# A Swin transformer block on one core: attention output and MLP moved one iteration later, new PSUM banks and engine orders, bias vectors loaded as rows

## The reference

```python
xn = layernorm(x, ln1_w, ln1_b)
xw = windows(roll(xn, (-3, -3)))            # (1024 windows, 49 tokens, 192)
q, k, v = split(xw @ qkv_w + qkv_b)         # 6 heads
attn = softmax(einsum('bhqd,bhkd->bhqk', q, k) * 32 ** -0.5)
o = einsum('bhqk,bhkd->bhqd', attn, v)
x = x + roll(unwindow(o @ proj_w + proj_b), (3, 3))
h = gelu(layernorm(x, ln2_w, ln2_b) @ mlp_w1 + mlp_b1)   # 192 -> 768
out = x + (h @ mlp_w2 + mlp_b2)                          # 768 -> 192
```

## Time and profile before

| what | value |
|---|---|
| runs shown | 3042.38 us median of 3 |
| profiled execution | 3044.16 us, of it the span of its instructions 3042.4 us |
| granted TensorE clock over the span | 0.991 of full speed |
| PE busy | 2993.3 us, 98% |
| DVE / ACT / POOL busy | 78% / 76% / 55% |
| DMA | 26 GB/s mean, queue share 9.6% |
| chain that ended last | PE 97% |

### The profile page before, as it was taken

One profiled execution on the slowest core, in us unless ns is written; L12 is line 12 of the kernel. 1 busy time (PEld: TensorE's weight loads), 2 busy tenths in 40 slices (PEclk: granted clock), 3 DMA queues, 4 the chain that ended last, 5 costly groups with the idle time before them and its releaser, 6 DMA issues.

```text
span 3042.4 us, 114962 instructions
## 1 busy us (share of the span) xinstructions
PE 2993.3 (98%) x43444; PEld 2832.5 (93%) x43444; DVE 2376.1 (78%) x6416; ACT 2300.3 (76%) x4493; POOL 1669.4 (55%) x1934
## 2 busy tenths in 40 slices
PE   5999999999999999999999999999999999999998
PEld 5999999999999999999999999999999999999997
DVE  4778877887887788778778877887887788788775
ACT  2777777777777777777777777777777777777776
POOL 2555555555555555555555555555555555555553
PEclk7999999999999999999999999999999999999999
DMA  1000110010001001000100100010010001001100
GB/s 46 25 25 24 27 29 24 24 30 25 24 26 29 24 24 30 26 24 26 29 24 24 30 26 24 26 29 24 24 29 26 24 25 30 24 24 27 28 24 17
DMA packets 112146, 79.79 MB, mean 26 GB/s; under 512 B 10128, under 2 KB 111602, under 8 KB 112114
## 3 DMA queue, kind: packets, MB, share of 16 engines
q1 hardware_dynamic: 112114, 79.35, 9.6%
HBM read 40.78 MB, written 38.54 MB: 26 GB/s over the span
## 4 chain that ended last, share of the span: by engine, by line
PE 97%; SPq 1%; DVE 1%; ACT 0%; issue 0%; POOL 0%; DMA 0%; DVEq 0%; POOLq 0%; ACTq 0%
PE ps L822 34%; PE ps L825 17%; PE ps L898 6%; PE ps L930 5%; PE ps L852 5%; PE ps L899 5%; PE ps L949 4%; PE ps L900 4%; PE ps L903 4%; PE ps L904 4%; PE ps L785 3%; PE ps L915 2%; PE ps L793 2%; PE ps L918 1%; SPq L291 1%; PE ps L795 1%
## 5 line engine op out<-in xcount | busy, mean ns | idle before, releaser
L398 POOL TENSOR_TENSOR gl<-g,gh 128x392 fp32r<-128x392 f32 x768 | 788.6, 1052 | 251.4 <-ACT gh L687 251.3
L822 PE MATMUL ps<-zh,w 128*128 128x392 f32 x3072 | 711.2, 346 | 0.6 <-ACT zh L649 0.6
L822 PEld LDWEIGHTS ps<-zh,w 128*128 128x128 f32 x3072 | 532.4, 188 | 31.4 <-ACT zh L649 0.9
L268 POOL TENSOR_TENSOR prob<-prob,rcp 128x588 f32<-128x588 f32 x128 | 152.4, 1190 | 537.4 <-DVE rcp L577 537.4
L681 ACT ACTIVATE g<-ps,biasf 128x392 f32<-128x392 f32 x768 | 389.3, 574 | 2.8 <-PE ps L822 2.8
L432 DVE BATCH_NORM_STATS2 st<-xin 98x6 f32<-98x192 f32 x512 | 145.9, 348 | 313.9 <-DMA xin<-in_x 313.6
L371 POOL TENSOR_TENSOR xb<-xin,projbv 98x768 f32<-98x768 f32 x128 | 234.5, 1832 | 284.3 <-DVE z L445 264.8
L687 ACT ACTIVATE gh<-g 128x392 fp32r<-128x392 f32 x768 | 365.0, 533 | 0.0
L822 PE MATMUL ps<-zh1c,wqkv 128*128 128x392 f32 x1536 | 358.4, 342 | 0.0
L825 PE MATMUL ps<-wqkv,zh 128*114 128x192 f32 x2048 | 290.8, 270 | 0.0
L898 PE MATMUL ps<-gh,w2h 128*128 128x392 f32 x768 | 288.7, 376 | 0.2 <-ACT pt L746 0.2
(11 more groups left out here) (107 smaller groups left out, 7406.5 us busy)
## 6 DMA issues: line engine op xcount, KB each, us to landing
xin<-in_x SPq DMA_DIRECT2D x128, 147.0 KB
out<-yo SPq DMA_DIRECT2D x128, 147.0 KB
xin<-in_x SPq DMA_DIRECT2D x128, 71.2 KB
out<-yo SPq DMA_DIRECT2D x128, 71.2 KB
xin<-in_x SPq DMA_DIRECT2D x128, 54.8 KB
out<-yo SPq DMA_DIRECT2D x128, 54.8 KB
xin<-in_x SPq DMA_DIRECT2D x128, 18.8 KB
out<-yo SPq DMA_DIRECT2D x128, 18.8 KB
```

The source lines that it names most:

```text
L398: pool.tensor_tensor(gl[:, m, :], g[:, m, :], gh[:, m, :].bitcast(F32), ALU.subtract)\
L822: last = pe.matmul(dst, cols(w, part), act_, start=(n == 0), stop=(n == 4))
```

## The change

The MLP of a group moves from the iteration after its attention to the second one after (`prev = i - 2` in all bodies), and pv, proj, the residual and the second norm move into the iteration after the scores (`mixes(i)`, for group i-1). `iterations` runs `range(5)` unrolled, then the loop, and one more iteration at the end (129 bodies before, 130 after). mlp2 is one unbroken run. The PSUM banks are dealt anew. Vectors are loaded as rows of 128 elements and turned into columns by two PE transposes; the weights are loaded from ACT's queue.

```diff
-        QK = (7, 1, 6)
-        V = 2
+        QK = (3, 4, 2)
+        V = 4
         S = (4, 5, 0, 1)
         T2 = 6
-        H = (4, 5, 2, 3, 7, 6)
-        Y = (4, 5)
-        TY = (2, 3)
+        H = (0, 1, 4, 5, 6, 7)
+        Y = (6, 7)
+        TY = (6, 7)
         T1 = 0
-        TP = (4, 2)
+        TP = (2, 4)
         PV = 2
         PROJ = (2, 3)
...
@@ PE body
-                prev = i - 1
+                prev = i - 2
                 if attends(i):
                     s(i)
+                if mixes(i):
+                    pv(i - 1)
                 if feeds(i):
                     wait(pe, z2_done, 1, prev, 1)
-                    wait(pe, x2_done, 2, prev, 2)
+                    wait(pe, yo_done, 2, prev - 1, 2)
                     transposes2()
                 if attends(i):
                     v(i)
+                if mixes(i):
+                    proj(i - 1)
                 if feeds(i):
                     mlp1(prev)
                 if attends(i):
                     turn_probs(i)
                 if more(i):
                     wait(pe, z1_done, 1, i + 1, 1)
                     wait(pe, s_sub, 2, i, 2)
+                    if feeds(i):
+                        wait(pe, g_done, KC, prev, 2)
                     transposes1()
                 if feeds(i):
-                    mlp2(prev, (0, 1), (0, 1))
-                if attends(i):
-                    pv(i)
-                if feeds(i):
-                    mlp2(prev, (2, 3), (2, 3))
-                    mlp2(prev, (4,), ())
-                if attends(i):
-                    proj(i)
-                if feeds(i):
-                    mlp2(prev, (5,), (4, 5))
+                    mlp2(prev)
                 if more(i):
+                    wait(pe, pt_ready, 2, i, 2)
                     qk(i + 1, (2,))
                     qk(i + 1, (1, 0))
                 if feeds(i):
                     turn_result(prev)
@@ waits inside the PE's helpers
 v:            -wait(pe, yo_done, 2, i - 2, 2)   +wait(pe, s_sub, 2, i, 1)
 s:            -wait(pe, yT_ready, 1, i - 2, 1)  -wait(pe, yTb_ready, 1, i - 2, 1)
 mlp1, m == 0: -wait(pe, s_sub, 2, prev + 1, 1)  +wait(pe, s_sub, 2, prev + 2, 2)
 mlp2:         +wait(pe, g_done, KC, prev, KC)   (ahead of its first matmul)
 turn_probs:   half 0 +wait(pe, x2_done, 2, i - 1, 2); half 1 +wait(pe, g_done, KC, i - 2, 4)
 turn_result:  wait(pe, yTb_ready, 1, prev, 1) now ahead of the second transposes only
...
@@ DVE body, the order after (helpers as before)
+ scores(i, 0); ol and oh of i-1 (after oh_ready of i-1); scores(i, 1)
+ low_wide2(i-2); low_narrow2(i-2); row_sums(i, 0); row_sums(i, 1); normalise(dve, i, 1)
+ residual(i-1); apply1(i+1); statistics of norm 2 (i-1); stats1(i+2); low_parts1(i+1)
+ norm 2 applied (i-1); queries_45(i+1); narrow_result(i-2); result(i-2)
@@ POOL body, the order after
+ normalise(pool, i, 0); gelu_parts(i-2); rstd of norm 2 (i-1); pad_windows(i+1)
+ rstd of norm 1 (i+2); add_proj_bias(i+1)
@@ ACT body, the order after
+ oh (i-1); exponential(i, 0); high_parts2(i-2); values(i); exponential(i, 1)
+ gelu(i-2, 0..3); high_gelu 0, 1; gelu 4, 5; high_gelu 2..5; pt (i); high_parts1(i+1)
+ narrow_result, wide_result (i-2); keys_45, heads_0123 (i+1)
...
@@ ahead of the loop: SP
-            load_weight(QKV, raw_qkv, qkv_w)
-            load_norm(lnw[:, 0, :], ln1_w, weight_loaded[QKV])
...
+            split_row(rows1, 2, ln1_b, rows1_loaded)
+            row(rows1[4:7, :], qkv_b, 0, [[C, 3], [1, A]], rows1_loaded)
...
+            row(rows2[4:4 + KC, :], mlp_b1, 0, [[128, KC], [1, 128]], rows2_loaded)
...
@@ ahead of the loop: ACT
+            load_weight(QKV, raw_qkv, qkv_w)
+            load_weight(PROJ_W, raw_proj, proj_w)
+            load_weight(W1, raw_w1, mlp_w1)
@@ ahead of the loop: PE and DVE
+            def columns(n, rows, loaded, count):            # PE
+                pe.wait_ge(loaded, 16 * count)
+                k = rows.shape[0]
+                pe.transpose(ps[:, VEC_BANKS[n], 0:k], rows[:, :], ident[0:k, 0:k]).then_inc(cols_mm, 1)
+            def columns(n, dst):                            # DVE
+                dve.wait_ge(cols_mm, n + 1)
+                dve.tensor_copy(dst[:, :], ps[:, VEC_BANKS[n], 0:dst.shape[1]]).then_inc(cols_ready, 1)
-            dve.wait_ge(consts_loaded, 16 * NCONST)
+            dve.wait_ge(projb_loaded, 16)
-            pe.wait_ge(projb_ready, 1)
```

More of the change, by code:

```diff
@@ L244, in iterations @@
         def iterations(eng, body, last=GROUPS - 4):
-            for i in range(3):
+            for i in range(5):
                 body(i, i % 2)
[L249 to L252, removed]
+            with eng.Fori(0, (last - 4) // 2) as j:
+                body(j * 2 + 5, 1)
+                body(j * 2 + 6, 0)
+            for i in range(last + 1, GROUPS + 2):
                 body(i, i % 2)
@@ L407, in body @@
             def body(i, parity):
+                if attends(i):
+                    normalise(pool, i, 0)
+                if feeds(i):
+                    gelu_parts(i - 2)
+                if mixes(i):
+                    rstd(mv2, ve2, rs2, mv2_done, ve2_done, rs2_done, i - 1, z2_done)
+                if more(i):
+                    pad_windows(i + 1)
+                if more(i + 1):
+                    rstd(mv1, ve1, rs1, mv1_done, ve1_done, rs1_done, i + 2, z1_done)
                 if more(i):
@@ L505, in low_weight @@
                 last.then_inc(w_lo, 1)
+            columns(0, cols1)
             stats1(0, 0)
             apply1(0, 0)
-            low_weight(QKV, [(lo, raw, hi, lnw[:, 0, part:part + 1]) for part in range(2)
+            low_weight(QKV, [(lo, raw, hi, lnw[0][:, part:part + 1]) for part in range(2)
                              for (raw, lo), (_, hi) in zip(qkv_pieces(raw_qkv[:, part, :], wqkv[:, 2 * part + 1, :]),
@@ L741, in body @@
                     high_gelu(prev, 1)
+                    gelu(prev, 4)
+                    gelu(prev, 5)
+                    for m in range(2, KC):
+                        high_gelu(prev, m)
                 if attends(i):
@@ L774, in body @@
                     heads_0123(i + 1)
+                if isinstance(i, int) and i == 1:
+                    act.wait_ge(bias_ready, 2)
             iterations(act, body)
@@ L889, in mlp1, with mlp2 @@
                     chunk(m, range(5)).then_inc(h_done, 1)
-            def mlp2(prev, high, low):
+            def mlp2(prev):
                 wide, narrow = ps[:, Y[0], 0:M], ps[:, Y[1], 0:M]
-                for k in high:
-                    if k == 0 and attends(prev + 1):
-                        wait(pe, pt_ready, 2, prev + 1, 1)
+                wait(pe, g_done, KC, prev, KC)
+                for k in range(KC):
                     wait(pe, gh_done, KC, prev, k + 1)
@@ L900, in mlp2 @@
                     pe.matmul(narrow, w2s[:, k, :], gh[:, k, :], start=(k == 0), stop=False)
-                for k in low:
+                for k in range(KC):
                     wait(pe, gl_done, KC, prev, k + 1)
@@ L937, in pv @@
                 wait(pe, pt_ready, 2, i, 2)
+                wait(pe, v_ready, 1, i, 1)
                 pe.nop(nofuse=True)
@@ L995, in body @@
                     mlp1(prev)
-                else:
-                    pe.wait_ge(weight_loaded[W1], 16 * LOADS[W1])
-                    pe.wait_ge(consts_loaded, 16 * NCONST)
-                    offsets(1, raw_w1, [(HID0 + k, 0, 128 * k, 128) for k in range(KC)])
-                    pe.wait_ge(bias_ready, 2)
                 if attends(i):
```

252 lines of the change are left out of this document (123 added, 129 removed).

## The result

| | before | after |
|---|---|---|
| median of the runs | 3042.24 us (3041.28 to 3042.52, 4 runs) | 3138.49 us (3135.26 to 3139.91, 4 runs) |
| ratio | | 1.0314 [1.0302, 1.0327] |
| profiled execution, span | 3044.16, 3042.4 us | 3139.02, 3137.2 us |
| steady period, s to s | 23.17 us | 23.83 us |

A forecast was written before the change was run, and what follows sets the result against it. PE, 98% busy, bounds the kernel; after the change PE waits for yTb. Period 22.85 + 0.9 + 0.25 = 24.0 us; ends 110.9 + 126 periods (3024) = 3135 us, whole range 2965 to 3200.

The forecast's parts named there:

- P without a quarrel: Steady iteration, s to s, if DVE and POOL don't hold each other up: 22.9 us, 0.26 better than before.
- 2.82. No wait, with nothing to spare: PE's v, due 2.86 us after s starts, waits for the next scores, expected ready at 2.82: no wait.
- The turns: DVE and POOL taking turns at SBUF: three casts cost norm 2's z 0.9 us, plus 0.25, per iteration.
- The slip of `gl`: Norm 1's z meets POOL's first gl, which makes the gl slip by 0.2 us; the sum adds 0.25.
- The ends: Everything outside the 126 steady periods: 64.5 us up to s(2) plus 46.4 from iteration 128's start, 110.9 us.
- s(0) at 23: Start of the first scores on PE: at 23 us instead of 40.12, with rows landed by 8, weights by 9.5.
- the break-even: The period P at which the kernel after would take as long as the kernel before: 23.26 us.
- Rival 1: POOL doesn't hold up DVE's norm z: P 22.9, 2996 us, or 2960 with s's 0.18 gone; chance 0.39.
- Rival 2: POOL's power (rs, 1.02 us) holds DVE's z too: 0.8 us more, P 24.8, 3236 us; chance 0.15.
- Rival 3: z yields to casts once or twice only, or the meeting moves: P 23.2 to 23.5, 3034 to 3072; chance 0.10.
- Rival 4: Vector rows and the split of the ends do nothing: s(0) stays near 40, every case 17 us later; no chance given.
- The meeting of norm 1 with `gl`: Norm 1's z behind POOL's gl makes transposes1 0.1 to 1.1 us late, hidden under the later wait for yTb.

The follow-up runs named there:

- f1: Kernel after, with POOL's wait for z2_done moved up ahead of the casts, so they follow DVE's six z; all work done: 3041.20 us, ratio 0.9994.
- e2: Kernel after, with the three casts in the loop cut to the first of eight windows (49 columns), the other work left out: 3042.45 us, ratio 0.9999.
- e1: Kernel after, with POOL's rstd of norm 1 (its power) moved ahead of the three casts, beside the six z: 3203.68 us, ratio 1.0527.
- h1: Kernel after, with norm 1's power directly behind norm 2's, beside the six z, and the casts held back until these are done: 3040.82 us, ratio 0.9999.
- e5: Kernel before, with only vectors loaded as rows, weights issued by ACT and PE's wait for projbv moved to the first v: 3032.61 us, ratio 0.9967.
- e3: Kernel after, with DVE's queries_45 and narrow_result moved ahead of norm 2's six z: 3064.82 us, ratio 1.0073.
- b1: Kernel before, with POOL's casts moved behind rstd of norm 2, so that they run beside DVE's six z: 3128.44 us, ratio 1.0283.
- g1: Kernel after, with nine iterations unrolled ahead of the loop instead of five: 3141.98 us, ratio 1.0327.

## Why the prediction was right, and where its terms were off

**The mechanism: right.** The power released both queues at once, the six `z` took longer beside the casts, and turn_result's second half waited for `yTb` in 126 iterations, 0.91 us each (forecast 1.2). f1 removes the meeting and 97 us with it.

**P without a quarrel: 22.9 forecast, 23.06 measured** (f1, e2). pv behind s and the end of the 0.22 before turn_result came as worked out. The term that failed is "2.82. No wait, with nothing to spare": the scores' subtraction ends 2.90 after the start of s (1513.68 + 0.77), v's first load is at 3.02 and not at 2.86, and v waits 0.25 in each iteration. s also waits 0.24 on average, not 0.18.

**The turns: 1.15 forecast, 0.77 measured.** The casts cost the six 0.77 and not 0.9, 0.26 for each of the three (0.3 was taken from the earlier trace rows). That 0.3 was so near is in part luck: it is the price of another DVE operation, beside which the casts themselves took 1.24, while here they keep 0.52 and DVE alone pays. Even for the same pair e1 shows 0.65 and 1.16 for the three. The slip of `gl` by 0.25 did not come: the four `z` of norm 1 give way wholly (2.01), and six `gl` take 5.99. Together P is 23.83, not 24.0: 126 x 0.17 = 21 us that the forecast has too much.

**The ends: 110.9 forecast, 3137.2 - 126 x 23.83 = 134.6 measured.** This is the step that failed, by 24 us, and it hid the 21 of the period, which was luck. Three terms:
- The start, 9.4 short: s(2) begins at 73.91 and not at 64.5. "s(0) at 23" was 29.40, 6.4 of it; iteration 0 took 24.33 and not 22, iteration 1 20.18 and not 19.5. I had the rows landed by 8 and weights by 9.5; ACT issues nine DMAs before it does anything else, the rows' transpose loads at 9.86 and the first offsets at 14.28, and ACT's first work is its table load at 16.69. Its queue, and PE's start:

```profile
4.76 3.91 ACTq L720 DMA_DIRECT2D raw_w<-in_L_conv_mlp_w  x1
...
11.91 4.68 ACTq L731 DMA_DIRECT2D w<-in_L_conv_mlp_w  x1
16.69 1.28 ACT L711 ACT_TABLE_LOAD   x1 [16.69 <-issue]
```
```profile
9.86 0.18 PEld L981 LDWEIGHTS ps<-ident,rows 9*128 9x128 f32 x1 [9.86 <-issue]
14.28 0.50 PEld L819 LDWEIGHTS ps<-cols,raw_qkv 128*128 128x128 f32 x2 [4.25 <-issue]
```
- The gaps in iterations 3, 4, 125 and 126, with the lower clock behind three of them: the 126 intervals between the starts of iterations 2 and 128 take 3015.4, and 126 x 23.83 is 3002.6: 12.8 us that no row of before showed.
- The tail, 1.5: 47.9 from the start of iteration 128, forecast 46.4.

9.4 + 12.8 + 1.5 = 23.7, less 21.4 for the period: 2.3 above 3134.9. The total was nearer than its terms deserved. What it cost in the judgement is the break-even: I put it at P = 23.26, it is (3042.4 - 134.6) / 126 = 23.08. Rival 1 promised 2996 without the quarrel; f1, which is that case, took 3041.

**The signs.** Of what the prediction said it would see, the wait for `yTb`, the period within 0.2 and the tail of 44 to 49 came. Outside are: the six `z` at 2.40 (2.5 to 3.3 forecast), the casts, which are not stretched, the wait at v, 0.25 (under 0.1), and s(0) at 29.40 (18 to 28).

**The rivals.** Rival 1 did not happen in the kernel after, and f1, which makes it happen, refutes its time. Rival 2 did not happen either: in the kernel after the last three `z` have their own length beside the power, and in h1 the power alone costs them nothing; e1's stretched `z` under it stay unexplained. Rival 3 had the number of stretched `z` right, two, but its period of 23.2 to 23.5 was too low: the first of them met two casts. The meeting of norm 1 with `gl` hides under the later wait, as argued. Rival 4 is refuted: s(0) moved by 10.7 us, and e5 shows what that is worth.

In the prediction I cited the Trainium skill, "SBUF — State Buffer", section "Who interferes with whom": the two engines exclude each other for a whole instruction. With casts and `gl` the trace agrees that the `z` stands until the other is over (a `z` begun with a `gl` at 1523.69 took 1141 ns where its neighbours take about 374, and ended 0.11 behind the `gl`). For the power, which that sentence would have made hold DVE as well, h1 disagrees.

## What to carry to other kernels

When a reordering lets one semaphore release DVE and GpSimd at the same moment, write down what the two will run side by side, and price every GpSimd operation on the DVE operation beside it before the order is built. Here the stretch landed on DVE and appeared as the PE's wait for `yTb`, an innocent instruction two places further on. If the second engine has slack, try a wait that keeps it back: here that (f1) gave back more than reordering the first engine (e3). And a deeper pipeline has to earn its fill and drain: here one more group of depth gave 0.11 us in each iteration, which the longer ends took back (134.6 against 3042.4 - 126 x 23.17 = 123.0), while a shorter start and one small wait of the shallow kernel gave 24 us. Where an experiment changes two neighbours at once (e1), it takes one run for each alone to say which of them paid.

## What the runs showed of the hardware that was not expected

- Who loses depends on the pair. Beside DVE's `z` (tensor_scalar), POOL's casts keep 0.52 to 0.55 and DVE pays for them, 0.23 (b1) or 0.26 (the kernel after) for each. Beside DVE's subtractions for the weights, in iteration 0 of the kernel after as in the earlier trace rows, the cast stretches, and DVE too: its `w2s` there takes 0.87, and 0.55 in the kernel before, where no cast runs at the time.

```profile
45.95 1.15 POOL L385 CAST zh<-zh1c 128x392 fp32r<-128x392 f32 x1 [9.94 <-DVE zh1c L449]
```
- A power over 98x4 elements, 1.02 to 1.09 us of POOL, costs DVE's `z` nothing (h1); with casts queued behind it some of the `z` under it are 0.19 to 0.28 longer (e1). Casts of 49 columns, 0.23 us each, cost them nothing that can be seen (e2).
- The long waits in pv (1.2 to 2.6 us, "issue") stand in iterations 3, 4, 125 and 126 of the kernel after and in 3, 4, 7, 10 and 125 of g1, and nowhere in the kernel before. Behind three of the four in the kernel after the granted clock falls to 0.50 or 0.66, and the iteration averages 0.88 or 0.94; iteration 125 has 1.00. Their cause was not found.
